# One launch of a windowed-attention network: the tensor engine's order of work in a strip, with four merged phases of small matmuls

## The reference, cut to what matters

```
x3 = concat(conv9x9(relu(x)), relu(x))            # 8 images, 56 x 56 tokens, DIM = 160
for shift, mask in ((0, None), (3, MASK1)):       # two Swin blocks, 7 x 7 windows, 5 heads of 32
    h = LN(x3); qkv = windows(roll(h)) @ qkvw + qkvb
    attn = softmax(q @ k.T * 32**-0.5 + bias (+ mask))
    x3 = x3 + roll_back(attn @ v @ projw + projb)
    x3 = x3 + gelu(LN(x3) @ w1 + b1) @ w2 + b2     # 160 -> 640 -> 160
y = x3 @ linw + linb; out = conv1x1(concat(conv9x9(y), y))
```

## Time and profile before

| what | value |
| --- | --- |
| median of three runs | 3065.28 us (3061.45 to 3066.93) |
| profiled execution, its own time | 3060.49 us |
| span of its trace | 3059.0 us (1.5 us lie around it) |
| mean granted PE clock | 0.989 of full speed |
| PE, PEld, DVE, ACT, POOL busy | 97%, 88%, 73%, 56%, 27% of the span |
| one body, first block / second block | 40.54 us / 43.85 us |

### The profile page before, as it was taken

How to read it: one execution, slowest core, us unless ns; L and a number is a source line. 1 busy time by engine, 2 the same in 40 slices (tenths; PEclk the granted TensorE clock), 3 DMA queues, 4 the chain that set the end, 5 groups by cost and what they waited for, 6 DMA issues and landing times. The chain is left out here.

```text
span 3059.0 us, 103594 instructions
## 1 busy us (share of the span) xinstructions
PE 2954.3 (97%) x39898; PEld 2702.5 (88%) x39898; DVE 2236.5 (73%) x6736; ACT 1719.2 (56%) x4076; POOL 837.3 (27%) x1470
## 2 busy tenths in 40 slices
PE   8889999999999999999999999999999999999799
PEld 6679999999999999999898989898999899898799
DVE  5667777777777777777777787778777777777522
ACT  6456656666656656666555655565556555655321
POOL 8122222222222222222332233223322332232110
PEclk9989999999999999999999999999999999999899
DMA  6411111111111111113111111111111111112274
GB/s 150 151 59 41 37 36 39 28 37 39 39 39 39 34 39 39 26 39 94 45 37 32 33 40 34 32 34 40 34 29 37 40 34 27 40 40 42 50 138 81
DMA packets 210424, 147.29 MB, mean 48 GB/s; under 512 B 15954, under 2 KB 205205, under 8 KB 210331
## 3 DMA queue, kind: packets, MB, share of 16 engines
q1 hardware_dynamic: 207619, 142.41, 19.9%
q10 hardware_dynamic: 1008, 3.44, 0.4%
q0 software_dynamic: 1728, 0.48, 0.1%
HBM read 95.64 MB, written 52.50 MB: 48 GB/s over the span
## 5 line engine op out<-in xcount | busy, mean ns | idle before, releaser
L1567 PE MATMUL rm<-w,ht 128*112 128x160 f32 x4480 | 681.9, 301 | 0.0
L1567 PEld LDWEIGHTS rm<-w,ht 128*112 128x112 f32 x4480 | 614.4, 177 | 4.4
L1051 POOL TENSOR_TENSOR rs<-ln_tmp,mhalf 112x4 f32<-112x4 f32 (+1 forms) x128 | 119.3, 932 | 1600.5 <-DVE ln_tmp L1223 1600.4
L1141 ACT ACTIVATE ht<-rm 128x448 f32<-128x448 f32 (+1 forms) x448 | 226.3, 505 | 146.7 <-PE rm L147 146.7
L1106 ACT ACTIVATE vb<-ra 113x320 f32<-113x320 f32 x256 | 113.1, 442 | 278.4 <-PE ra L147 276.8
L1009 POOL TENSOR_TENSOR z<-z,one 112x448 f32<-112x448 f32 (+2 forms) x192 | 131.6, 685 | 339.7 <-DVE z L1227 339.7
L1270 DVE TENSOR_TENSOR sc<-so,tabs 113x490 f32<-113x490 f32 x256 | 171.3, 669 | 54.5 <-PE so L1511 42.1
L147 PE MATMUL rm<-z2t_hi,w_hi 128*128 128x448 f32 (+1 forms) x448 | 167.4, 374 | 35.4 <-DVE z2t_rest L1331 32.6
L1534 PEld LDWEIGHTS so<-vb,pt 49*49 49x49 f32 x10240 | 143.0, 123 | 60.0 <-issue 54.7
L1287 DVE RECIPROCAL rd<-so 113x10 f32<-113x10 f32 x256 | 56.0, 219 | 190.7 <-PE so L1534 183.1
L1123 ACT ACTIVATE ot_hi<-ra 128x98 fp32r<-128x98 f32 x512 | 103.2, 260 | 151.2 <-PE ra L1546 149.8
(11 more groups left out here) (278 smaller groups left out, 9242.8 us busy)
## 6 DMA issues: line engine op xcount, KB each, us to landing
xa<-xs SPq DMA_DIRECT2D x128, 245.0 KB
xr<-xs SPq DMA_DIRECT2D x128, 245.0 KB
xs<-xo SPq DMA_DIRECT2D x64, 245.0 KB
ys<-yz SPq DMA_DIRECT2D x64, 245.0 KB
c_y<-ys SPq DMA_DIRECT2D x36, 260.0 KB
xs<-a_tok SPq DMA_DIRECT2D x14, 560.0 KB, 6.3
xs<-tok_late SPq DMA_DIRECT2D x14, 560.0 KB, 6.5
a_nat<-in_x ACTq DMA_DIRECT2D x7, 480.0 KB, 5.4
```

The lines of the kernel that those rows point to most:

```text
L1141: act_(ht[:, f * SN + t0 * TT:f * SN + (t0 + nt) * TT], bank_m(i, lm, use)[:, 0:nt * TT], ACT.Gelu_apprx_tanh).then_inc(m_freed(i, lm, use ...
L1567: last = mm(bank_m(i, lm, use)[0:TT, t * DIM:(t + 1) * DIM], ht[:, c:c + TT], keep.w["w2", lm][:, f * DIM:(f + 1) * DIM], start=(f == 0), ...
```

## The change

The order of phase B is written anew on PE, ACT, DVE and POOL. No matmul, activation or vector operation is added or taken away in a steady body. On PE a strip is now: mlp_turned(0), outputs(0) with scores(2), weights_turned(1), values(3), G0 to G2, mlp_turned(1), G3, G4, outputs_turned(0), outputs(1) with scores(3), G5 to G9, outputs_turned(1), (linear in the second block), front_turned(0), W0, weights_turned(2), front_turned(1), W1, Q0, K0, B0, W2, outputs(2) with scores(0) of the next strip, weights_turned(3), values(0), values(1), outputs_turned(2), outputs(3) with scores(1) of the next strip, weights_turned(0) of the next strip, W3, outputs_turned(3), W4, the projections, Q1, B1, W5, K1, values(2). An `outputs` and the `scores` two groups on now stand side by side; DVE reads `so` for `outputs(j)` only when both are written. DVE splits the maximum from `scores_less_max`; the statistics and normalisation of the input (`xa`) run one strip earlier; `normalise` of half 1 of z2 moves to the next body; the second block's linear comes ahead of W0; banks and slots are dealt out anew.

```diff
-        FRONT = ["T1A0", "T1C0", "T1A1", "T1C1", "Q0", "K0", "B0", "V0", "Q1", "V1", "K1", "V2", "V3", "B1"]
+        FRONT = ["T1A0", "T1C0", "T1A1", "T1C1", "Q0", "K0", "B0", "V0", "V1", "Q1", "B1", "K1", "V2", "V3", "OT0"]
         PRO = Ring(FRONT, 3, {})
-        RA = Ring(["T1A0", "T1C0", "T1A1", "T1C1", "OT0", "Q0", "K0", "OT1", "B0", "V0", "Q1", "OT2", "V1", "OT3", "K1",
-                   "P0", "P1", "P2", "V2", "V3", "B1", "T2A1", "T2C1"], 3, {})
...
+        RA = Ring(["OT1", "T1A0", "T1C0", "T1A1", "T1C1", "Q0", "K0", "B0", "V0", "V1", "OT2", "OT3", "P0", "P1", "P2",
+                   "Q1", "B1", "K1", "V2", "V3", "T2A1", "T2C1", "OT0"], 3, {})
+        END = Ring(["OT1", "OT2", "OT3", "P0", "P1", "P2", "T2A1", "T2C1"], 3, {})
...
-        T2_LIN = [("T2A0", 0), ("T2C0", 2)]
-        RM0 = Slots(T2)
-        RM = [Slots(MLP_USES + T2), Slots(MLP_USES + LIN_USES + T2_LIN)]
+        T2_USES = [("T2A0", 1), ("T2C0", 0)]
+        G_USES = [(f"G{g}", n) for g, n in enumerate((2, 1, 0, 2, 1, 0, 1, 2, 0, 1))]
+        L_USES = [("L0", 2), ("L1", 0), ("L2", 1), ("L3", 2)]
+        W_USES = [(f"W{n}", n % 2) for n in range(len(PAIRS))]
...
+                def turned_rest(hf):
+                    pool.wait_ge(s_norm[1], 2 * i + hf + 1)
+                    repeat_rest(z2, s_z[1], *HALF[hf])
+
+                if la is not None:
+                    power(0)
+                    turned_rest(0)
+                    power(1)
+                    if la == 1:
+                        pool.wait_ge(*m_freed(i, lm, "L3" if lm == 1 else "W5"))
+                        base_second(i, 0, *HALF[0])
+                    turned_rest(1)
+                    if la == 1:
+                        base_second(i, 1, *HALF[1])
...
@@ -1106,91 +1112,94 @@
...
+                if lm is not None:
+                    t_hi(0)
+                if la is not None:
+                    weights_out(1, i)
+                    values(3, m)
...
+                if lm is not None:
+                    gelu(0)
+                    gelu(1)
+                    gelu(2)
+                if lm is not None:
+                    t_hi(1)
+                    gelu(3)
+                    gelu(4)
+                if la is not None:
+                    outputs_hi(0)
+                if lm is not None:
+                    gelu(5)
+                    gelu(6)
+                    gelu(7)
+                    gelu(8)
+                    gelu(9)
+                if la is not None:
+                    outputs_hi(1)
+                    exps(2, i)
                 if ln is not None:
                     front_hi(0)
                 if la is not None:
...
+                    weights_out(2, i)
                 if ln is not None:
                     front_hi(1)
                 if la is not None:
...
+                    exps(3, i)
                 if ln is not None:
                     queries(0)
...
+                    keys(0)
+                    fifth_head(0)
+                if la is not None:
+                    weights_out(3, i)
                 if ln is not None:
...
                     values(0, i)
...
+                    values(1, i)
                 if la is not None:
                     outputs_hi(2)
                 if ln is not None:
...
+                    exps(0, i + 1)
+                    weights_out(0, i + 1)
                 if la is not None:
                     outputs_hi(3)
                 if ln is not None:
+                    exps(1, i + 1)
+                    queries(1)
+                    fifth_head(1)
                     keys(1)
                     values(2, i)
...
 
             bodies(act, body)
...
@@ -1284,6 +1296,8 @@
                     dve.wait_ge(s_of, n)
+                    if j < 2 or ln is not None:
+                        dve.wait_ge(s_sfull, n + 2)
                     v.reciprocal(view(rd, 0, QP, 0, [[HEADS, 2], [1, HEADS]]),
                                  view(so, 0, QP, OC + HD, [[512, 2], [VW, HEADS]])).then_inc(s_rec, 1)
...
+                if la is not None:
+                    scores_biased(2, i, la)
+                    scores_max(2, i)
+                    scores_less_max(2, i)
+                if lm is not None:
+                    dve.wait_ge(s_pow, 2 * m + 2)
+                    normalise(1, z2, x1, *HALF[1])
                 if lm == 1:
...
+                    reach(dve, *linear_freed(i))
                     v.reciprocal(std[:], rs[1][:]).then_inc(s_std, 1)
...
+                if la is not None:
+                    outputs(0)
+                if lm is not None:
+                    t_lo(1)
+                if la is not None:
+                    outputs_lo(0)
+                if la is not None:
+                    scores_biased(3, i, la)
+                    scores_max(3, i)
+                    scores_less_max(3, i)
+                    outputs(1)
+                    outputs_lo(1)
+                if lm == 1:
+                    for n in range(len(LPAIRS)):
+                        linear_out(n)
+                if more:
+                    xa_stats(i + 2)
                 if ln is not None:
                     front_lo(0)
...
                 if ln is not None:
                     front_lo(1)
...
+                if lm is not None:
+                    mlp_out(0)
+                if more:
+                    xa_normalised(i + 2)
+                if lm is not None:
+                    mlp_out(1)
                     mlp_out(2)
                 if la is not None:
...
                     outputs(2)
+                if ln is not None:
+                    scores_biased(0, i + 1, ln)
+                    scores_max(0, i + 1)
+                    scores_less_max(0, i + 1)
+                if la is not None:
+                    outputs_lo(2)
                     outputs(3)
...
+                if ln is not None:
+                    scores_biased(1, i + 1, ln)
+                    scores_max(1, i + 1)
                 if la is not None:
                     outputs_lo(3)
                 if lm is not None:
...
+                    mlp_out(3)
+                if ln is not None:
+                    scores_less_max(1, i + 1)
+                if lm is not None:
+                    mlp_out(4)
                 if la is not None:
                     dve.wait_ge(s_xr, 32 * (i + 1))
                     reach(dve, s_x1b, i)
...
                     residual(0)
                     residual(1)
                     x1_stats(0, False)
                     x1_stats(1, True)
                     variance(i, 0)
...
@@ -1497,7 +1523,7 @@
                     reach(pe, s_sadd, n * NG + j)
-                    reach(pe, s_od, n * NG + {0: 0, 1: 0, 2: 0, 3: 1}[j])
+                    reach(pe, s_od, n * NG + j - 2)
                     pe.nop(nofuse=True)
                     for b in range(HEADS):
...
@@ -1512,20 +1538,19 @@
+                def weights_turned(j, n):
+                    pe.wait_ge(s_exp, n * NG + j + 1)
+                    reach(pe, s_pte, n * NG + j)
+                    if lm is not None and j == 2:
+                        pe.wait_ge(*m_freed(i, lm, "G7" if lm == 0 else "L3"))
...
                     reach(pe, s_od, i * NG + j)
                     pe.nop(nofuse=True)
...
                         room_m(use)
+                        if g % FT == 0:
+                            pe.wait_ge(*turned_freed(i, lm, f"T2A{hf}"))
+                            pe.wait_ge(*turned_freed(i, lm, f"T2C{hf}"))
+                        if la is not None and g == 0:
+                            pe.wait_ge(s_pte, i * NG + 2)
                         last = split_passes(nc, bank_m(i, lm, use)[:, 0:nt * TT], *[t[:, t0 * TT:(t0 + nt) * TT] for t in z2t],
...
+                def mlp_turned(hf):
+                    pe.wait_ge(s_z[1], 2 * m + hf + 1)
+                    turn(z2, hf, lambda u: turned_bank(i, lm, u), lambda u: turned_room(i, lm, u),
+                         lambda u: turned_full(i, lm, u)[0], "T2")
+
+                if lm is not None:
+                    mlp_turned(0)
+                if la is not None:
+                    outputs(0)
+                    scores(2, i)
+                    weights_turned(1, i)
+                    values(3, m, la)
+                if lm is not None:
                     mlp_in(range(3))
...
+                if lm is not None:
+                    mlp_turned(1)
                     mlp_in(range(3, FT))
                 if la is not None:
...
+                    outputs_turned(0)
+                    outputs(1)
+                    scores(3, i)
+                if lm is not None:
                     mlp_in(range(FT, 2 * FT))
...
+                if la is not None:
+                    outputs_turned(1)
+                if lm == 1:
+                    linear(range(len(LPAIRS)))
                 if ln is not None:
                     front_turned(0)
...
+                if lm is not None:
+                    mlp_out(0)
```

(22 more changed lines are left out.)

356 lines of the change are left out of this document (115 added, 241 removed).

## The result

The changed kernel takes 3162.6 us (median of 4 runs, 3160.6 to 3166.3) against 3063.9 us (3061.5 to 3066.9): ratio 1.0325, 95% interval 1.0313 to 1.0337. It is slower, as forecast, but by 99 us and not by 25, outside the range. The profiled execution's span is 3161.1 us, 102.1 more than before, at a mean granted clock of 0.983 (0.989 before).

The account below looks back on a forecast made before the run. It took PE to bound the kernel, busy nearly all of each body. 32 x 0.61 + 31 x 0.25 + 2 = 29 us on the profiled 3060.5 gave 3089.8, forecast as 3090 us, range 3058 to 3118.

Parts of the forecast that it names:

- the merging carries through: Whole body: waits stay under 2.0 us, bodies take 38.6 and 41.4 us, 2930 us in all; chance of this side 0.15.
- a wash: Whole body: the predicted waits are overrated by 0.3 to 0.6 us a body, giving 3059 to 3071 us; chance 0.13.
- Steps 1 to 5 and 7 to 9: All stretches of PE's first-block body except Q0 to values(1), each the later of PE's arrival and its producer's chain.
- steps 2: PE from mlp_turned(0) to mlp_turned(1): 6.12 us, with a wait of 0.4.
- 9 (2.29): PE from outputs_turned(3) to projection(0): 2.27 us, with a wait of 0.5.
- step 5: PE from weights_turned(2) to Q0: 3.03 us, with a wait of 0.6.
- step 3: PE from mlp_turned(1) to outputs_turned(1): 7.6 us through gelu(4) and DVE's division of outputs(1), with a wait of 0.55.
- step 6: PE from Q0 to values(1): 6.25 us, no wait, with 0.05 for the boundary between outputs and scores.
- The third rival: Inside merged phases: a full way in and out is paid; 16 us more, 3106 us; chance 0.12.
- Edits costed at nothing: Earlier input statistics, SP's transfers, POOL's base operations and ACT's table loads were taken to add no time.
- Prologue and end: First and last strips: about 3.2 us bare in the last strip, less what was lost there before; +2 us, bounds 0 and 5.
- The fourth rival: DVE's dense order from outputs(2) on: one late operation delays the next three consumers; 0.5 us more a body, 3121; chance 0.08.

Follow-up runs that it names:

- e10_divide_earlier: Changed kernel with DVE's division of outputs(1) ahead of the low part of outputs_turned(0) and the biases of scores(3); 3123.3 us, ratio 1.0202.
- e7_unmerged: Changed kernel with outputs_turned(0) moved between outputs(1) and scores(3), so one merged phase is two again; 3206.0 us, ratio 1.0463.
- e6_fewest_waits: Changed kernel with four waits fewer ahead of scores behind outputs, one kept of three for Q, K and B; 3139.8 us, ratio 1.0247.
- e8_three_repairs: Changed kernel with margins copied image by image, strip 1's statistics last in the first body, POOL's repeat ahead of base_second(0); 3128.3 us, ratio 1.0209.
- e12_all_repairs: Changed kernel with fewest waits, earlier division, front, repeat and normalise, spread margins, later taps, strip 1's statistics last; 3030.7 us, ratio 0.9896.
- e1_start: Changed kernel with DVE's statistics and normalisation of strip 1's input last in the first body; 3157.6 us, ratio 1.0308.
- e11_before_one_wait: Kernel before the change, with one wait in place of three ahead of scores(0) and scores(2); 3061.7 us, ratio 0.9995.
- e4_repeat_first: Changed kernel with POOL's repeat of half 1 of z2 ahead of base_second(0) in the second block; 3147.7 us, ratio 1.0279.

## Why the prediction was wrong, by its own steps

**Right: the direction, and the walk of waits.** The rival that the merging carries through is refuted, and so is a wash. Steps 1 to 5 and 7 to 9 measured within 0.2 us; steps 2 (6.24) and 9 (2.29) lie where they were put, step 5 (2.84) is 0.2 shorter. And e10_divide_earlier, which takes 0.5 us out of step 3's chain at the link the walk names, shortens the strip by 0.6. The clock is 1.00 in steady bodies of both blocks. With 0.4 us taken off for the boundary, and 0.4 more in the second block for DVE beside POOL, strips are about 0.6 and 0.35 us longer than before, where 0.61 and 0.25 were predicted: the direction was no luck.

**Right: a merge is worth 0.3 us, and the boundary inside one can be nearly free** (0.03 measured between outputs(1) and scores(3), 0.05 taken; 0.27 on PE in e7_unmerged). TensorEngine Tiling (Array Packing), Key Properties, of the Trainium skill: by that rule the change of tile costs no drain, and the trace agrees with its 0.48 us for 40 matmuls that take 0.45.

**Wrong: the boundary in step 6.** It was costed at 0.05 from the array's even step alone; it costs 0.50 (0.95 - 0.45), of which e6_fewest_waits takes 0.42 away by removing four waits. The third rival had a size of this kind (0.25) but the wrong mechanism: nothing drains; PE's queue works off five waits in the open. The step lacked a term for instructions that are not matmuls, and the sum put the other three places down as filled waits. Over 62 strips it is 0.4 x 62 = 25 us.

**Wrong: "Edits costed at nothing", in three of its sentences.** They carry most of the miss.

- "The statistics and normalisation of `xa` a strip earlier: ... their transfer are needed some 15 us after they are issued": true of a steady body, not of the two places where SP has other transfers ahead of that load. At the change of blocks it costs 24.4 us (e8_three_repairs takes 14.9 of them by spreading the margins' copies, e12_all_repairs, with a 45.0 us interval, more by moving the taps; its neighbours are 40.2, so 4.8 remain), and at the start 4 to 5.6 (e1_start, e8_three_repairs).
- "Prologue and end ... +2 us, bounds 0 and 5": +19.9 and about -7.6. Besides the transfer it is the new order of the first bodies, in which PE is idle 8.6 us more for want of data: 10.7 us at like clocks (e1_start at 0.75 against e11_before_one_wait at 0.74). What is left, 1 to 3 us, goes with the lower granted clock (an estimate by difference). Which of PE's waits there make up the 10.7 was not taken apart.
- "base_second(0) ends before half 1 is normalised": it does, by 0.45 us, and still costs 0.4 us a strip in the second block, 0.4 x 31 = 12 us, because it holds up DVE's less_max, which stands ahead of the normalise (e4_repeat_first). The sentence asked when POOL would be free and not what its operation runs beside. The fourth rival, a late operation of DVE that is passed on, had the size (0.5) and another place, outputs(2) and behind.

**Mis-sized.** Steps 1 and 2 of the first block by 0.1 each, step 5 by -0.2 the other way; together under 0.1 us a strip.

These terms account for it: 24.4 + 19.9 - 7.6 for the two ends and the middle, 25 for the boundary, 12 for POOL and DVE are 74 us, on top of the 27 predicted for the steady strips: 101 of the 102.1 us.

## What to carry to other kernels

When an order is changed, walk the steady body, and then walk the first body, the last and every place where one queue has an extra job (here SP's copies and tap loads): a load that is wanted one body earlier is late there and nowhere else. Between short phases count the waits as work: a phase of 0.45 us hid about one record of them here, so drop those that an earlier wait implies, or put a long phase there. Put at nothing only an operation whose neighbours in time on the other engines have been looked at too. And a new order can be right while its consumers' own engines still have the old one: one swap on DVE (e10_divide_earlier) gave back 0.6 us a strip, over a third of this loss.

## What the runs showed of the hardware that was not expected

- PE's queue takes about 0.1 us for each record of a wait with a computed value, and gets hardly ahead of small matmuls with it: outputs to scores take 0.95, 0.73, 0.63, 0.53 and 0.48 us with six, four, three, two and one record. Where scores stand behind larger matmuls, dropping waits gains nothing (e11_before_one_wait, 0.9995).
- DVE's subtraction with both inputs in SBUF takes 1.06 us or more beside POOL's addition, 0.67 alone; DVE's operations with one input in PSUM keep their time beside it.
- The stretch from the first transpose to the first projection, of the same instructions, took 53.5 us at a granted clock of 0.75 and 56.2 at 0.65.
